# A gated graph network on one core: TensorE's loop written out, and both low parts of `a` ahead of the second turn of the state

## What is computed

```
h = max(layernorm(x), 0)                       # x: 128 graphs x 64 nodes x 256 features
q, k, v = h Wq^T, h Wk^T, h Wv^T               # attention over the nodes of a graph
rel = adj^T * (q k^T);  rel = rel / norm(rel over the keys)
x = x + rel v
h = max(layernorm(x), 0)
repeat 3 times:                                # gated graph network
    a  = adj h                                 # a_in = a_out, both use adj
    z  = sigmoid([a, a] w3 + h u3 + biases)
    r  = sigmoid([a, a] w4 + h u3 + biases)
    hv = tanh([a, a] w5 + (r h) u5 + biases)
    h  = (1 - z) h + z hv
x = x + h
```

## Time and profile before

| | us |
|---|---|
| median of 3 runs | 914.64 |
| lowest, highest | 911.21, 915.95 |
| the profiled execution | 917.08 |
| its span from first to last instruction | 915.3 |
| PE busy | 881.5 (96%) |
| DVE busy | 750.6 (82%) |
| ACT busy | 493.4 (54%) |
| PE's mean granted clock | 0.979 |

### The profile page before, as it was taken

How to read it: one execution, slowest core, us unless ns; L and a number is a source line. 1 busy time by engine, 2 the same in 40 slices (tenths; PEclk the granted TensorE clock), 3 DMA queues, 4 the chain that set the end, 5 groups by cost and what they waited for, 6 DMA issues and landing times.

```text
span 915.3 us, 19786 instructions
## 1 busy us (share of the span) xinstructions
PE 881.5 (96%) x7356; PEld 718.7 (79%) x7356; DVE 750.6 (82%) x1518; ACT 493.4 (54%) x881; POOL 122.3 (13%) x161
## 2 busy tenths in 40 slices
PE   8999999899998999989999899998999899999997
PEld 7878788687886878868788687877888688878886
DVE  5988979688896888968989679897888968899666
ACT  5464646456364464645645456355555555555553
POOL 1210112102021020210202101121011300112000
PEclk9999999899998999989999899999999999999998
DMA  5022324413344142441524514255141542315122
GB/s 180 24 83 80 109 101 145 157 47 116 103 150 140 47 138 93 138 140 47 161 70 138 163 47 140 69 159 164 52 136 47 176 149 69 116 61 171 71 69 93
DMA packets 88466, 99.76 MB, mean 109 GB/s; under 512 B 8641, under 2 KB 80577, under 8 KB 88385
## 3 DMA queue, kind: packets, MB, share of 16 engines
q1 hardware_dynamic: 88384, 98.50, 33.9%
HBM read 50.76 MB, written 47.71 MB: 108 GB/s over the span
## 4 chain that ended last, share of the span: by engine, by line
PE 69%; issue 14%; DVE 10%; ACT 3%; POOL 3%; DMA 1%; DVEq 0%; SPq 0%; POOLq 0%; ACTq 0%
PE gate L439 10%; PE cand L434 8%; PE gate L434 8%; PE cand L435 7%; PE cand L436 7%; PE gate L435 7%; PE gate L436 7%; PE fea L594 4%; DVE c_s L1190 2%; PE fea L524 2%; POOL rstd L379 2%; PE tok L434 2%; PE tok L435 1%; PE tok L436 1%; PE fea L434 1%
## 5 line engine op out<-in xcount | busy, mean ns | idle before, releaser
L870 ACT ACTIVATE r_s<-gate,b_r 128x512 f32<-128x512 f32 x96 | 60.8, 685 | 106.0 <-PE gate L439 106.0
L883 ACT ACTIVATE z_s<-gate,b_z 128x512 f32<-128x512 f32 x96 | 63.9, 683 | 68.2 <-PE gate L436 68.1
L434 PE MATMUL cand<-a_hi,W_hi_w 128*128 128x512 f32 x192 | 80.5, 419 | 19.8 <-issue 19.8
L1185 DVE SCALAR_TENSOR_TENSOR d_s<-z_s,h 128x512 f32<-128x512 f32 x96 | 63.5, 686 | 42.3 <-ACT z_s L883 42.3
L379 POOL TENSOR_TENSOR rstd<-vare,minus_half 128x4 f32<-128x4 f32 x32 | 41.9, 1311 | 325.7 <-DVE vare L1030 325.7
L776 ACT ACTIVATE h_hi<-h 128x512 fp32r<-128x512 f32 x92 | 57.1, 631 | 52.2 <-DVE h L996 31.9
L1222 DVE TENSOR_TENSOR rh<-r_s,h 128x512 f32<-128x512 f32 x96 | 66.4, 732 | 18.7 <-ACT r_s L870 17.5
L434 PE MATMUL gate<-h_hi,W_hi_u 128*128 128x512 f32 x192 | 80.3, 418 | 0.3 <-DVE h_lo L996 0.3
L436 PE MATMUL cand<-a_hi,W_lo_w 128*128 128x512 f32 x192 | 79.8, 416 | 0.0
L435 PE MATMUL cand<-a_lo,W_hi_w 128*128 128x512 f32 x192 | 79.8, 415 | 0.0
L776 ACT ACTIVATE rh_hi<-rh 128x512 fp32r<-128x512 f32 x96 | 58.2, 631 | 38.8 <-DVE rh L1222 38.8
(11 more groups left out here) (154 smaller groups left out, 2055.7 us busy)
## 6 DMA issues: line engine op xcount, KB each, us to landing
h_back<-h_trip SPq DMA_DIRECT2D x216, 128.0 KB, 2.8
h_trip<-h_turned SPq DMA_DIRECT2D x40, 512.0 KB, 2.6
x_s<-x SPq DMA_DIRECT2D x15, 512.0 KB, 5.1
out<-o_s SPq DMA_DIRECT2D x15, 512.0 KB, 4.5
hx_back<-hx_trip SPq DMA_DIRECT2D x56, 128.0 KB, 2.8
h_trip<-h_blk SPq DMA_DIRECT2D x14, 512.0 KB, 3.1
hx_trip<-hx SPq DMA_DIRECT2D x14, 256.0 KB, 3.0
hx_trip<-hx SPq DMA_DIRECT2D x28, 128.0 KB, 2.8
```

The costliest lines, as they stand in the source:

```text
L434: nc.tensor.matmul(dst, l_hi, r_hi, start=start, stop=False, skip_group_check=True)
L870: nc.scalar.activation(r_s[:, c, :], gate[:, c, :], ACT.Sigmoid, bias=b_r[:, c:c + 1]).then_inc(r_ready, 1)
L883: nc.scalar.activation(z_s[:, c, :], gate[:, c, :], ACT.Sigmoid, bias=b_z[:, c:c + 1]).then_inc(z_ready, 1)
L1185: nc.vector.scalar_tensor_tensor(d_s[:, c, :], z_s[:, c, :], 1.0, h[s][:, c, :], ALU.subtract, ALU.mult).then_inc(diff_ready, 1)
```

## The change

It has two parts. In PE's program the loop is gone: a Python loop writes its body out seven times, with the semaphore values as constants, and `first_reset_gate` becomes the head of window 1 (the order of the products stays as it was). The increments of `sources_seen` go as well. In DVE's `update` the subtraction for the second set, `split_a(w, s, 1)`, moves ahead of the second half's transpose, `turn_half(w, o, 1)`. The loops of the other engines stay.

```diff
             def weighted_sum(n_v, n_rel):
                 tok_done(n_v)
                 pe.wait_ge(fea_taken, 2 * n_rel + 2)
-                pe.sem_inc(sources_seen, 1)
...
                     if t_full is not None:
                         pe.wait_ge(t_ready, t_full + c)
-                    if c == 0 or t_full is not None:
-                        pe.sem_inc(sources_seen, 1)
...
-            def first_reset_gate(i):
-                pe.wait_ge(h_lo_new, 4 * i + 4)
-                reset_gate_h(6 * i + 1, 1)
-                reset_gate_a(6 * i + 1, 1, use_in_round("adj 0", i - 1))
-
             def window(i, k, use, attention=True, new=True):
...
                 if k == 0:
                     pe.wait_ge(h_lo_new, 4 * i + 2)
-                elif k > 1:
+                elif k == 1:
+                    pe.wait_ge(h_lo_new, 4 * i + 4)
+                else:
                     pe.wait_ge(h_lo_ready, 8 * i + 2 * (k - 1))
-                if k != 1:
-                    reset_gate_h(w, s)
-                    reset_gate_a(w, s, use("adj %d" % (k - 1)) if k else use_in_round("adj 5", i - 1))
+                reset_gate_h(w, s)
+                reset_gate_a(w, s, use("adj %d" % (k - 1)) if k > 1 else use_in_round("adj 0" if k else "adj 5", i - 1))
...
-            first_reset_gate(0)
-            with pe.Fori(0, PAIRS - 1) as i:
+            for i in range(PAIRS - 1):
                 for k in (1, 2, 3, 4, 5):
                     window(i, k, lambda name: use_in_round(name, i))
                 window(i + 1, 0, lambda name: use_in_round(name, i))
-                first_reset_gate(i + 1)
...
                 split_a(w, s, 0)
+                split_a(w, s, 1)
                 turn_half(w, o, 1)
-                split_a(w, s, 1)
```

More of the change, by code:

```diff
@@ L187, in gated_graph_kernel @@
         tok_taken = sem("tok_taken")
-        sources_seen = sem("sources_seen")
         h_is_turned, h_out, h_in, t_ready = sem("h_is_turned"), sem("h_out"), sem("h_in"), sem("t_ready")
```

## The result

| | before | after |
|---|---|---|
| median of the runs, us | 915.02 (4 runs, 911.21 to 915.95) | 880.28 (4 runs, 878.96 to 880.94) |
| profiled execution, us | 917.08 | 878.96 |
| span, us | 915.3 | 877.2 |
| mean granted clock | 0.979 | 0.999 |

The medians are 34.7 us apart. In the profiled executions the difference is 38.1 us, where the prediction's sum says 39.7.

A forecast was written before the change was run, and what follows sets the result against it. The prediction took PE's own order of work to bound the kernel. From the profiled 917.08 us, less 35.8, less 4.5, plus 0.6, it got 877.4 and predicted 877.0 us, range 871 to 888.

The forecast's parts named there:

- the main case of the forecast: PE has no idle time at the round boundaries and the clock stays at 1.00; 877.0 us, chance 0.78.
- its own signs of being wrong: A PE gap of about 3 us, PE waiting for t_s or rh_lo after the boundary, or a lowered clock mid-run.
- the first rival: At the round's boundary t_s, rh_lo or the new a_lo comes 0.9 to 1.6 us late; 882 to 886, chance 0.13.
- Six back edges at 35.8 us: PE's loop end: removing six taken jumps cuts stretches totalling 98.06 us to 10.375 each, a gain of 35.8 us.
- the idle time isn't the jump's: PE's idle time belongs to the amount of code and turns up elsewhere; no gain from unrolling, about 912, chance 0.03.
- Idle time 20.6, lower clock 15.2: Split of the 35.8 us gain at PE's jumps: some 20.6 us idle time, 15.2 us products at the lower clock.
- Only the idle time goes: The lower clock comes back somewhere in each round; only 20.6 and 4.5 us are gained, 892 us, chance 0.04.
- Part two at 4.5 us: DVE's earlier second subtraction shortens PE's waits for a_lo; 4.5 us gained, bounds 0 to 5.4.
- The wait in window 4: PE's wait for a_lo in window 4 of each round disappears; 0.52 us seven times, 3.6 us.
- 0.1 us a boundary for rh_lo: Allowance for new PE waits at six round boundaries (rh_lo, a_lo, t_s); 0.6 us in all, bounds 0 to 9.6.
- The later transpose and hx, cost nothing: DVE's second transpose ends 0.6 us later, delaying SyncE's trips; costed at nothing, hx blocks landing about when DVE needs them.
- From the profile to the median: Profiled execution before was 2.4 us above the median; only a small part carried over, taking 877.4 to 877.0.

The follow-up runs named there:

- b_unroll_alone: Kernel after, with DVE's old order of split_a and turn_half put back and PE's program still written out; 884.59 us, ratio 0.9646.
- c2_two_jumps: Kernel after, but PE loops three turns over two written-out rounds each, giving two taken back edges, with the increments kept; 893.67 us, ratio 0.9749.
- d_idle_no_jump: Kernel after, plus a PE wait for both halves of rh before candidate_a in window 1 of rounds 2 to 8, no jump; 915.27 us, ratio 0.9968.
- g_load_later: Kernel after, with SyncE's load of x for the round's second group moved behind the trip of hx; 877.5 us, ratio 0.9578.
- g_again: Repeat of the kernel after with the load of x behind the trip of hx, timed beside the unchanged kernel after; 877.75 us, ratio 0.9605.
- e_idle_short: Kernel after, plus a PE wait for both halves of r before candidate_a in window 1 of rounds 2 to 8; 884.3 us, ratio 0.9655.
- after_again: Kernel after, unchanged, timed again later beside the version with the load of x behind the trip of hx; 883.32 us, ratio 0.966.

## Why the prediction was right, and where it wasn't

The time is inside the range, and the main case of the forecast is the one that came: no idle time at the jump, no lower clock. Of its own signs of being wrong one did show: PE waits for rh_lo just after the round's boundary. It is the first rival in small, 0.22 to 0.45 us late where that one had 0.9 to 1.6. By the steps:

- **Six back edges at 35.8 us.** Confirmed to a tenth where it stands alone: six stretches of 62.17 us in `b_unroll_alone`, 6 x 10.375 = 62.25 in the prediction. The loop's entry and exit were the right yardstick, the number of jumps is what counts (`c2_two_jumps`), and "the idle time isn't the jump's" is out. In time the kernel with part one alone is 33.6 us below the runs beside it (32.5 by the ratio); the a_lo waits, new in window 2 and longer in window 4, take some 3 us back.
- **Idle time 20.6, lower clock 15.2.** The split was right, and that the second follows from the first is shown by `d_idle_no_jump`. "Only the idle time goes" is out.
- **Part two at 4.5 us.** Behind part one it is between nothing and 4.3 us by the runs and 2.6 to 4.6 by the traces, so the size isn't confirmed. The wait in window 4, 3.6 us of the term, is gone in four of seven rounds, not in all. Alone part two is 13.9, which the prediction did not see, since it left the jump's idle time out of what DVE's order could touch. I had called the later transpose free; in the kernel with the jump it was a gain, as it moved 512 KB of traffic off the fetch of code. For the sum this had no weight, because the jump was gone.
- **0.1 us a boundary for rh_lo.** This term is mis-sized. PE starts candidate_rh 0.22 to 0.45 us late at the six boundaries, 2.2 us in all where 0.6 stands in the sum (the bounds, 0 to 9.6, hold it). One of them, in the kernel after:

```profile
172.19 0.47 PE L433 MATMUL cand<-rh_hi,W_hi_u 128*128 128x512 f32 x1 [0.29 <-DVE rh_lo L986]
```

  The working set rh_lo's end, 284.88, against a PE that starts candidate_a at 279.6, the time of the old order. Part two lets PE start sooner, and leaves the end of DVE's two operations, and all that comes behind, where it was. In `b_unroll_alone`, with the old order, there is no such wait. The margin belonged to part one and was counted for both.
- **The later transpose and hx, cost nothing.** Half right. I put DVE and the blocks of hx at the same time; in round 3 of the kernel after DVE is free at 287.46 and hx lands 1.5 us later, and over an execution the wait comes to 11.0 us in seven rounds. Part one alone brings 5.6 us of it (`b_unroll_alone`), part two the rest:

```profile
286.76 0.70 DVE L1197 STREAM_TRANSPOSE h_turned<-h 128x512 f32<-128x512 f32 x1
288.96 1.30 DVE L1034 STREAM_TRANSPOSE hxT<-hx_back 128x512 f32<-128x512 f32 x2 [1.50 <-DMA hx_back<-hx_trip]
```

  This didn't reach PE in window 2 of the first profile, but PE still waits for a_lo in window 4 of three rounds, its group 0.4 to 0.7 us late, where the prediction had no wait left (one of them below), and in the repeat it costs whole microseconds. With the load of x behind the trip (`g_load_later`, `g_again`) these waits in window 4 are gone. I had named bunched traffic in a rival, but only for t_s.

```profile
218.31 0.39 PE L438 MATMUL gate<-a_hi,W_lo_w 128*128 128x512 f32 x1
219.21 1.21 PE L438 MATMUL gate<-a_lo,W_hi_w 128*128 128x512 f32 x4 [0.51 <-DVE a_lo L986]
```

- **From the profile to the median.** I went 0.4 us under the sum made from the profiled execution, since that stood 2.4 above the median of before. After the change the profiled execution was the fastest of four, 1.3 below their median. This step is 1.7 us off; with the 1.6 us that the rh_lo term was too small it makes the 3.3 us between 877.0 and 880.28. What varies between executions now is traced in two of them only: the time ahead of the loop and how late hx is.

Open is what decides whether the clock falls after an idle time of some 2 to 3 us. It fell all fourteen times after 3.13 to 4.63 us (the kernel before, `c2_two_jumps` and `d_idle_no_jump`), and held each of the seven times after 0.9 (`e_idle_short`) and once after 1.51 (`after_again`, before the queries). It fell once after 1.78, and in seven of twelve cases after 2.40 to 2.93, among them shorter ones than some after which it held. It was also not tried whether GpSimd's, ACT's, DVE's or SyncE's loops pay for their jumps; none showed a gap that another engine waited for.

## What to carry to other kernels

A loop on the engine that bounds a kernel can cost far more than its branch: look in that engine's row for an idle time with no releaser at the same place in every round, and for slowed products behind it, and measure both against a pass through the same code without the jump. Where two changes meet at one place, work out each margin with the other change already in, for the engine that gets earlier and for the one that doesn't. And once a stall is gone, look at the transfers that lay under it: here one load moved behind a trip gave another 5.6 us where the two were timed side by side, a sixth of the main gain, for no work at all.

## What the runs showed of the hardware that I had not expected

- A fetch of PE's code shares the DMA engines with the kernel's own traffic: with a 512 KB write ahead of it the jump's idle time is 3.13 to 3.42 us, with the write held back 2.63 to 2.89, and the time of the whole is 8.6 us less.
- A taken back edge of PE costs 3.1 to 4.6 us of idle time over a body of one or two rounds. Over a body of four small products it costs at most some 0.5 us, which is the spread of the same products without a loop.
- 0.9 us of idle time, seven times, and 1.51 us, once, left the granted clock at 1.00, while 1.78 us once lowered it for part of the stretch behind. Between 2.40 and 2.93 us it fell in seven of twelve cases, and the longer idle time wasn't always the one that lowered it.
